# A recurrence whose states lie between zeros, with products of 32 columns in place of 8

## The reference

```python
h = tok(x)                      # 8 x 64 x 1000 samples -> patches of 200, |rfft|, angle, MLP to 128 features
h = h + ssm(layernorm(h))       # 320 steps of a 32-wide tanh recurrence, batch 8
h = h + gru(layernorm(h))       # 320 steps of a 256-wide gated recurrence, batch 8

def step(h, inp):               # inside gru
    xz_t, xr_t, xc_t = inp
    z = sigmoid(xz_t + h @ Wwz.T + bwz)
    r = sigmoid(xr_t + h @ Wwr.T + bwr)
    c = tanh(xc_t + h * r @ Ww.T + bw)
    h_new = z * h + (1.0 - z) * c
    return (h_new, h_new)
out = sigmoid(hs @ Wo.T + bo)
```

## Time and profile before

| | us |
|---|---|
| median of 3 runs | 890.94 |
| the profiled execution | 889.93 |
| its span, first to last instruction | 888.1 |
| TensorE busy (matmul) | 831.7 (94%) |
| TensorE busy (weight load) | 704.6 (79%) |
| VectorE / ScalarE / GpSimd busy | 583.0 / 370.9 / 74.5 |

### The profile page before, as it was taken

The page is one execution under the profiler, slowest core; times in us unless marked ns, Lnnn a source line. Parts: engine busy times, 40 slices in busy tenths (PEclk is TensorE's granted clock), DMA queues, the critical chain, the costliest instruction groups (busy, mean ns, idle before and its releaser), DMA issues.

```text
span 888.1 us, 40652 instructions
## 1 busy us (share of the span) xinstructions
PE 831.7 (94%) x17111; PEld 704.6 (79%) x17111; DVE 583.0 (66%) x3495; ACT 370.9 (42%) x2016; POOL 74.5 (8%) x189
## 2 busy tenths in 40 slices
PE   8999999989999999999999999999999998988875
PEld 7677667778888888888888888888888887877765
DVE  5343538376777776767767777777677777676655
ACT  5565766433343443433434434334334343343322
POOL 3111102110000000100000001000000000000000
PEclk9979999955555555555555555555555555555555
DMA  7100000000000000000000000000000000000000
GB/s 172 38 1 0 1 1 1 2 3 3 7 3 6 7 3 6 7 3 6 4 6 7 3 6 7 3 6 4 7 6 4 6 7 3 6 6 3 7 3 8
DMA packets 7454, 8.53 MB, mean 10 GB/s; under 512 B 1343, under 2 KB 6557, under 8 KB 7271
## 3 DMA queue, kind: packets, MB, share of 16 engines
q1 hardware_dynamic: 6965, 5.92, 2.9%
q0 software_dynamic: 256, 0.01, 0.0%
q10 hardware_dynamic: 50, 0.00, 0.0%
HBM read 4.62 MB, written 1.31 MB: 7 GB/s over the span
## 4 chain that ended last, share of the span: by engine, by line
PE 85%; ACT 7%; DVE 4%; issue 3%; POOL 0%; POOLq 0%; DVEq 0%
PE ps L1527 42%; PE ps L1533 11%; PE ps L1340 8%; PE ps L1238 4%; PE ps L1440 3%; PE ps L1541 3%; PE ps L1404 3%; DVE h_hi L479 2%; PE ps L1448 2%; ACT addend L847 1%; PE ps L1322 1%; PE ps L1329 1%; PE ps L1310 1%; PE ps L1260 1%; PE ps L1254 1%
## 5 line engine op out<-in xcount | busy, mean ns | idle before, releaser
L1527 PE MATMUL ps<-h_hi,w_first 128*128 128x8 f16 x2552 | 267.6, 170 | 27.8 <-DVE h_hi L479 27.7
L1527 PEld LDWEIGHTS ps<-h_hi,w_first 128*128 128x128 f16 x2552 | 220.3, 104 | 89.8 <-DVE h_hi L479 89.8
L1527 PE MATMUL ps<-h_hi,w_rest 128*128 128x8 f16 x5104 | 275.8, 168 | 0.0
L1527 PEld LDWEIGHTS ps<-h_hi,w_rest 128*128 128x128 bf16 x5104 | 241.0, 105 | 0.1
L837 ACT ACTIVATE tanh_r<-ps 128x16 f32<-128x16 f32 x320 | 59.2, 185 | 250.2 <-PE ps L1533 249.7
L1533 PE MATMUL ps<-h_lo,w_first 128*128 128x8 f16 x2560 | 159.0, 168 | 0.1
L1527 PE MATMUL ps<-rh_hi,w_first 128*128 128x8 f16 x1276 | 136.0, 172 | 12.6 <-DVE rh_hi L1132 0.9
L1527 PEld LDWEIGHTS ps<-rh_hi,w_first 128*128 128x128 f16 x1276 | 109.0, 104 | 39.6 <-DVE rh_hi L1132 1.1
L1527 PE MATMUL ps<-rh_hi,w_rest 128*128 128x8 f16 x2552 | 138.6, 168 | 0.0
L479 DVE TENSOR_TENSOR_SCAN h_hi<-coef,addend 128x32 f16<-128x32 f32 x320 | 73.3, 229 | 83.7 <-ACT addend L847 83.7
L1527 PEld LDWEIGHTS ps<-rh_hi,w_rest 128*128 128x128 bf16 x2552 | 121.2, 105 | 0.0
(11 more groups left out here) (210 smaller groups left out, 1375.3 us busy)
## 6 DMA issues: line engine op xcount, KB each, us to landing
x_sb<-in_x SPq DMA_DIRECT2D x4, 500.0 KB
out<-res SPq DMA_DIRECT2D x20, 64.0 KB, 2.0
W_sb<-in_L_tok_W SPq DMA_DIRECT2D x1, 606.0 KB
W_sb<-in_L_tok_W SPq DMA_DIRECT2D x1, 384.0 KB
wnat<-in_L_ffn_Wwr SPq DMA_DIRECT2D x1, 256.0 KB, 5.5
wnat<-in_L_ffn_Wwz SPq DMA_DIRECT2D x1, 256.0 KB, 11.8
wnat<-in_L_ffn_Ww SPq DMA_DIRECT2D x1, 256.0 KB, 10.4
wunat<-in_L_ffn_Wur SPq DMA_DIRECT2D x1, 128.0 KB, 7.1
```

The costliest lines, as they stand in the source:

```text
L1527: mm(gate(c, j, g, m), w[:, m * 128:(m + 1) * 128], state[:, k * NB:(k + 1) * NB], start=False, stop=False, skip_group_check=True)
```

## The change

The four tiles of states get room for zeros: each is now 112 positions (`ROW`) long, the 16 states stand at positions 48 to 63, and all other positions are set to zero once. Within the 16 the order is now batch b, half k, so that the batch entries of one half are two positions apart. A product no longer moves the 8 columns of its step but 32 (`WIDE` = 4 steps): its own 8 and 24 zeros. For steps 0 to 12 of a chunk the zeros come behind and are added to the columns of the next three steps; for steps 13 to 15 they come ahead and are added to the columns of the last steps before. Number, order and weights of the products stay as they were. GpSimd sets two tiles more to zero at the start, and PE waits for that once, ahead of the recurrence (`consts`, 18).

```diff
+WIDE = 4
...
-        h_hi = sb("h_hi", [128, SW, 2], F16)
-        h_lo = sb("h_lo", [128, SW], F16)
+        SEG = WIDE * NB
+        PAD = SEG - NB
+        ROW = KH * (PAD + SEG)
+        h_hi = sb("h_hi", [128, ROW, 2], F16)
+        h_lo = sb("h_lo", [128, ROW], F16)
...
-        rh_hi = sb("rh_hi", [128, SW], F16)
-        rh_lo = sb("rh_lo", [128, SW], F16)
+        rh_hi = sb("rh_hi", [128, ROW], F16)
+        rh_lo = sb("rh_lo", [128, ROW], F16)
...
+        def states_of(tile):
+            return tile[:, KH * PAD:KH * SEG]
+
+        def moving(tile, k, j):
+            first = k + (KH * PAD if j + WIDE <= CH else 0)
+            cols = slice(first, first + KH * (SEG - 1) + 1, KH)
+            return tile[:, cols, 1] if tile is h_hi else tile[:, cols]
...
+            pool.memset(rh_hi[:], 0.0).then_inc(consts, 1)
+            pool.memset(rh_lo[:], 0.0).then_inc(consts, 1)
...
-                                 hseq[:, s0:s0 + CH // 2, :, 1].rearrange("p t (k b) -> p t k b", k=KH)
+                                 hseq[:, s0:s0 + CH // 2, :, 1].rearrange("p t (b k) -> p t k b", k=KH)
...
             def halves(tile):
-                return tile.rearrange("p (m b) -> p m b", m=KH)
+                return tile.rearrange("p (b m) -> p m b", m=KH)
...
-                    v.scalar_tensor_tensor(out=rh_hi[:], in0=tanh_r[:], scalar=1.0, in1=h_prev,
+                    v.scalar_tensor_tensor(out=states_of(rh_hi), in0=tanh_r[:], scalar=1.0, in1=h_prev,
...
-                    scan(v, h_hi[:].rearrange("p s i -> p (s i)")).then_inc(h_hi_done, 1)
+                    scan(v, states_of(h_hi).rearrange("p s i -> p (s i)")).then_inc(h_hi_done, 1)
...
             def gate(c, j, g, m):
-                return gate_columns(g, c)[:, m, j, :]
+                first = j if j + WIDE <= CH else j + 1 - WIDE
+                return gate_columns(g, c)[:, m, first:first + WIDE, :].rearrange("p t b -> p (t b)")
...
                             mm(gate(c, j, g, m), w[:, m * 128:(m + 1) * 128],
-                               state[:, k * NB:(k + 1) * NB], start=False, stop=False, skip_group_check=True)
+                               moving(state, k, j), start=False, stop=False, skip_group_check=True)
...
+            pe.wait_ge(consts, 18)
```

More of the change, by code:

```diff
@@ L1136, in body @@
                     dve.wait_ge(rh_full, t + 1)
-                    v.tensor_tensor(rh_lo[:], rh[:], rh_hi[:], ALU.subtract).then_inc(rh_lo_done, 1)
+                    v.tensor_tensor(states_of(rh_lo), rh[:], states_of(rh_hi), ALU.subtract).then_inc(rh_lo_done, 1)
                     dve.wait_ge(z_done, t + 1)
@@ L1154, in body @@
                     dve.wait_ge(h_full, t + 1)
-                    v.tensor_tensor(h_lo[:], hseq[:, j, :, 1], h_hi[:, :, 1],
+                    v.tensor_tensor(states_of(h_lo), hseq[:, j, :, 1], states_of(h_hi)[:, :, 1],
                                     ALU.subtract).then_inc(h_lo_done, 1)
@@ L1533, in recur_lo @@
                         last = mm(gate(c, j, g, m), w_first[:, g, k, m * 128:(m + 1) * 128],
-                                  state[:, k * NB:(k + 1) * NB], start=False, stop=k == KH - 1,
+                                  moving(state, k, j), start=False, stop=k == KH - 1,
                                   skip_group_check=True)
@@ L1562, in body @@
                     if not start_of_all:
-                        recur_hi(c, j, 0, h_hi[:, :, 1])
+                        recur_hi(c, j, 0, h_hi)
                     if not start_of_all:
                         pe.wait_ge(h_lo_done, t)
-                    recur_lo(c, j, 0, h_lo[:]).then_inc(r_psum, 1)
+                    recur_lo(c, j, 0, h_lo).then_inc(r_psum, 1)
                     if not start_of_all:
-                        recur_hi(c, j, 1, h_hi[:, :, 1])
-                    recur_lo(c, j, 1, h_lo[:]).then_inc(z_psum, 1)
+                        recur_hi(c, j, 1, h_hi)
+                    recur_lo(c, j, 1, h_lo).then_inc(z_psum, 1)
                     if scan_2 and j < CH - 1:
@@ L1575, in body @@
                     if not start_of_all:
-                        recur_hi(c, j, 2, rh_hi[:])
+                        recur_hi(c, j, 2, rh_hi)
                     pe.wait_ge(rh_lo_done, t + 1)
-                    recur_lo(c, j, 2, rh_lo[:]).then_inc(c_psum, 1)
+                    recur_lo(c, j, 2, rh_lo).then_inc(c_psum, 1)
                     if not out_before and j == LAST_ROWS_AT:
```

## The result

The changed kernel takes 917.33 us (median of three runs, 916.05 to 917.48), the kernel before 890.94: 1.0288 times as long, interval 1.0272 to 1.0303. The sign was forecast, the size wasn't: +12.6 us were expected, +26.4 came, and the time is above the range. The profiled execution is the median run itself, span 915.5 us against 888.1.

What follows compares the result with a forecast made beforehand. The prediction took a recurrence chain of 2.20 us a step as the bound. Profiled 889.93 us plus 12.8 for two group ends, all else 0, gave 902.7; 1.0 to the median made 903.7, stated as 903.5, range 882 to 907.

Steps and rivals of the forecast that it cites:

- the six links: One recurrence step's chain: scan, r's products, tanh, `rh_hi`, c's products, tanh; 2.20 us a step.
- Part one, 27 ns from product to product: State products on PE: with 32 columns they still start every 27 ns, unchanged, at 1.2 GHz.
- Part one, the end of the groups: Last product of r's and c's groups: 24 more columns cost 20 ns, twice a step, 12.8 us.
- the rivals' sum: Rival of a clock that rises and stays: ends cost 10 ns twice, 2.18 us a step, 883.3 us; chance 0.18.
- Part one's rival rule: Trainium skill on PE streams: 81 ns with loads against 56 without, some 25 ns per unhidden load; not used.
- Part two, the work behind c: Other PE work behind c's products: at most 20 ns in a few tens of steps, 0.5 us, left out.
- Part three, `h_hi` at 8 bytes taken at 0: Products reading `h_hi` 8 bytes apart, where it was 4: no cost, though no row shows that distance.
- the third rival: Products on PE outlast their load: 1210 us, or 1044 us if only the 8-byte read is half speed; chance 0.10.
- Part three, layout of ScalarE and VectorE at 0: ScalarE and VectorE accessing the states with halves interleaved: 0, bound 0 to 10 ns a step.
- GpSimd's memsets: Zeroing two more and two longer tiles at the start: 0.2 to 0.4 us of GpSimd, nothing in the time.
- The clock at half throughout: PE's granted clock stays 0.50 from the first recurrence steps to the end; with 20 ns twice, chance 0.52.
- comes and goes: Rival: recurrence clock full only in stretches, steps of 2.18 or 2.24 us, 894 us, between 886 and 902; chance 0.12.

Runs made afterwards that it cites:

- the first experiment: Changed kernel with the states' layout undone (high states read 4 bytes apart) and 32 columns a product kept: 893.01 us, 1.0026 of the kernel before.
- the fifth: The first experiment's kernel with 8 columns in all low products, four at the end of each group: 889.45 us, 1.0002 of the kernel before.
- sixth: The first experiment's kernel with 8 columns in only the last product of each group: 888.24 us, 0.9987 of the kernel before.
- seventh: The sixth's kernel plus products of 256 zero columns behind c's last, three without other work there, one with: 878.32 us, 0.9876 of the kernel before.
- experiments 1 and 3: 1 is the first experiment; 3 is the changed kernel with 24 columns a product: 902.06 us, 1.0124 of the kernel before.
- experiments 1 and 4: 1 is the first experiment; 4 is the changed kernel with `rh_hi` also read 8 bytes apart: 940.37 us, 1.0561 of the kernel before.
- Experiment 2: The changed kernel, new layout kept, with 8 columns a product: 895.13 us, 1.0047 of the kernel before.
- experiment 9: The seventh's kernel with 8 columns in every state product and six or four zero-column products a step: 1070.83 us, 1.2026 of the kernel before.
- experiment 7: The seventh: the sixth's kernel plus three or one products of 256 zero columns behind c's last: 878.32 us, 0.9876 of the kernel before.

## Why the prediction was wrong, step by step

- **What bounds the kernel, the six links: right.** The chain is the same; each link that grew did so by its own amount.
- **Part one, 27 ns from product to product: right for 4-byte operands, wrong for the rest.** `rh_hi`, `h_lo` and `rh_lo` keep 27 ns (25 at full clock) with 32 columns, and in the first experiment `h_hi` too. In the changed kernel its 24 products per step take 32. So one of the prediction's own signs came, a group of z longer than 0.42 us; another was the clock of 1.00 after 180 us.
- **Part one, the end of the groups: right.** 20 ns twice were forecast; from the last product's start to ScalarE's are 224 ns with 32 columns, 218 with 24 and 204 with 8, and the fifth and sixth take 40 and 34 ns off a step at half clock. At full clock it is 214 with 32 columns and 203 with 8 (seventh), 10 ns as the rivals' sum had it.
- **Part one's rival rule: rightly left out.** Loads aren't added to products in these runs: z's products of 32 columns, each with its load, start 26.7 ns apart at half clock and 25.0 at full in the first experiment.
- **Part two, the work behind c: right.** The mean of the steps at half clock is 9 ns above their median, 8 before.
- **Part three, `h_hi` at 8 bytes taken at 0: this is the step that failed.** With 32 columns it cost 50 to 54 ns a step at half clock (experiments 1 and 3), 17 us if it held for all 319 steps, more than the whole forecast. I knew that no row showed it, had 0 and the third rival's 0.48 us as its ends, and took the end that its nearest rows seemed to favour; but those rows are all of products read at 4 bytes or less, and none bears on the distance. The rival's mechanism was the true one with the wrong size: I had half speed of the clock in mind, 53 ns for 32 columns, and it is 32, 1.0 ns a column. Part three's sentence on the Trainium skill (Advanced Engine Details and Errata, section SBUF Cachelines) helped me to 0: two hits in 16 bytes should be enough for full speed. The runs disagree for what PE reads: at 8 bytes 32 columns took 32 ns where at 4 bytes they took 27 and 25 (experiments 1 and 4). At 24 columns nothing is lost, but there the load sets the distance, so that run can't tell.
- **Part three, layout of ScalarE and VectorE at 0 with 0 to 10 ns as the bound: too small.** The tanh of c costs 12 ns more, 14 by its own rows, 4 us in all. I set beside it the tanh of c before, which wrote every second float and took as long as one that wrote side by side; every fourth is another case. Experiment 2 has it alone, with 4 ns more in r's group: 4.2 us by its time against the kernel before, 6.4 by its 20 ns in 319 steps.
- **GpSimd's memsets: right.** The two new ones take 0.18 us each, and its last copy of the identity starts at 5.32 us; VectorE's first use is at 12.83. Its copy of the states, 115 ns longer, wasn't in the sum; it is off the chain.
- **The clock at half throughout: wrong.** The rival "comes and goes" had this with 0.12, and doubted it for the reason that the step idles. It gave back some 7 us. But it couldn't have made the change faster: a step wholly at full clock is 2.247 us in this kernel, 2.214 before at half.

Together: 12.8 for the ends, 17.2 and 3.8 for the two parts of the layout are 33.8 us. Measured over the steps are 26.75, and the steps with full clock account for 7.9 of the difference, somewhat more than there is. So two terms that the sum had at 0 were wrong with opposite signs, 21 us against 7 to 8; the sign of the result was forecast for the smaller of its causes, the ends of the groups.

## What to carry to other kernels

When a change moves data into another layout, price the distance at which each engine reads and writes it together with how much it reads: here the columns alone cost 2 us and the layout alone 4, and both together 26. Columns of a short product that stand under its weight load cost nothing here but at the end of a group, so keep the last product before a hand-over narrow. Padding can buy clock, but look at what a step is worth at full clock before paying for it: here 54 ns of 2213, and in the changed layout even a step at full clock was longer than one at half clock before.

## What the runs showed of the hardware

- A product of 32 float16 columns read 8 bytes apart takes 32 ns in a stream at both clocks, 26.7 and 25.0 at 4 bytes or less. At 24 columns and half clock nothing of it is seen. That it is 1.0 ns for each column is the simplest reading of these two widths; no other width above the load's time was run.
- With the next load beside them, products of 8 to 32 columns, read at 4 bytes or less, start every 26.7 ns at half clock; those of 32 start every 25.0 at full: doubling the clock is worth 6% there.
- The way of a result from the last product's start to ScalarE's is 204 ns at half clock and 203 at full with 8 columns, 224 and 214 with 32: only the columns' part follows the clock.
- ScalarE's tanh of 16 floats takes 185 ns written to every second float and 197 to 199 to every fourth. GpSimd's copy of 128 x 128 went from 293 to 408 ns when it read the halves interleaved.
- Columns that hold only zeros raised the clock (0.50 before, 0.68 in the first experiment), and PE's busy time doesn't tell when: 395 busy us of 400 stayed at 0.50 (experiment 9), 362 of 400 had 0.90 (experiment 7).
